# Per-subject projection with residual: loads and stores in one queue in a fixed order

## The reference

```python
def _L0_cond_ref(x, subjects, weights):
    B, C, D, T, N_SUBJECTS = (128, 128, 128, 1024, 8)
    w = weights[subjects]
    out = jnp.einsum('bct,bcd->bdt', x, w)
    return out
x = x + _L0_cond_ref(x, itok_B_0_7, L0_cond_weights)
```

## Time and profile before

| | us |
|---|---|
| median of 3 runs | 324.39 (323.96 to 324.61) |
| the profiled execution | 325.0 |
| its span | 323.2 |
| PE busy | 244.7 (76%) |
| DVE busy | 196.1 (61%) |
| ACT busy | 132.3 (41%) |

### The profile page before, as it was taken

One profiled execution on the slowest core, in us unless ns is written; L12 is line 12 of the kernel. 1 busy time (PEld: TensorE's weight loads), 2 busy tenths in 40 slices (PEclk: granted clock), 3 DMA queues, 4 the chain that ended last, 5 costly groups with the idle time before them and its releaser, 6 DMA issues.

```text
span 323.2 us, 3584 instructions
## 1 busy us (share of the span) xinstructions
PE 244.7 (76%) x1024; PEld 113.0 (35%) x1024; DVE 196.1 (61%) x261; ACT 132.3 (41%) x131; POOL 0.8 (0%) x7
## 2 busy tenths in 40 slices
PE   0599999788868787666996869868668768698640
PEld 0244444343434333333442334434324323344320
DVE  3278888863766755577184773737765547736360
ACT  4045646632434434244152442424443424424240
POOL 1000000000000000000000000000000000000000
PEclk9999999997989999999697998979999979989785
DMA  8999999999999999999999999999999999999994
GB/s 285 422 420 396 431 424 427 428 424 431 426 428 431 423 431 427 425 431 425 431 429 424 431 426 427 432 423 431 427 425 431 425 430 429 424 431 424 428 430 196
DMA packets 17975, 134.80 MB, mean 417 GB/s; under 512 B 1073, under 2 KB 1586, under 8 KB 1586
## 3 DMA queue, kind: packets, MB, share of 16 engines
q1 hardware_dynamic: 9232, 67.64, 50.0%
q10 hardware_dynamic: 8738, 67.11, 49.1%
HBM read 67.63 MB, written 67.11 MB: 417 GB/s over the span
## 4 chain that ended last, share of the span: by engine, by line
DMA 62%; PE 27%; DVEq 2%; DVE 2%; issue 2%; ACT 1%; ACTq 0%; SPq 0%
DMA out<-x_ring 40%; PE product L211 27%; DMA x_ring<-x 21%; DVEq L123 2%; DMA weight_halves<-weights 1%; DVE x_ring L132 1%; DVE x_ring L131 0%; DVEq L44 0%; ACT weight_bank L160 0%; DVE weight_ring L124 0%; ACT x_ring L169 0%; DVE weight_bank L117 0%; DVEq L124 0%; ACTq L187 0%; SPq L81 0%
## 5 line engine op out<-in xcount | busy, mean ns | idle before, releaser
L211 PE MATMUL product<-x_ring,weight_ring 64*128 64x512 f32 x1024 | 244.7, 632 | 66.3 <-DMA x_ring<-x 49.5
L211 PEld LDWEIGHTS product<-x_ring,weight_ring 64*128 64x128 f32 x1024 | 113.0, 200 | 197.2 <-issue 140.1
L131 DVE TENSOR_TENSOR x_ring<-product,x_ring 64x1024 f32<-64x1024 f32 x64 | 77.9, 1217 | 104.3 <-PE product L211 104.3
L168 ACT COPY x_ring<-product 64x1024 f32<-64x1024 f32 x64 | 64.5, 1008 | 176.3 <-PE product L211 176.3
L132 DVE TENSOR_TENSOR x_ring<-product,x_ring 64x1024 f32<-64x1024 f32 x64 | 78.6, 1228 | 0.8
L169 ACT COPY x_ring<-product 64x1024 f32<-64x1024 f32 x64 | 64.2, 1003 | 0.8
L124 DVE COPY weight_ring<-weight_bank 64x256 f32 x128 | 36.9, 288 | 7.1 <-issue 4.3
L111 DVE COPY weight_bank<-weight_halves 64x1024 f32<-64x1024 f32 x2 | 1.4, 688 | 4.8 <-DMA weight_halves<-weights 4.8
L160 ACT COPY weight_bank<-weight_halves 64x1024 f32<-64x1024 f32 x2 | 2.2, 1123 | 2.3 <-DMA weight_halves<-weights 2.3
L160 ACT ACT_TABLE_LOAD x1 | 1.3, 1283 | 1.4 <-PEq L229 1.4
L117 DVE TENSOR_TENSOR weight_bank<-weight_bank,eye 64x512 f32<-64x512 f32 x2 | 1.4, 687 | 0.3 <-ACT weight_bank L160 0.2
## 6 DMA issues: line engine op xcount, KB each, us to landing
x_ring<-x SPq DMA_DIRECT2D x32, 2048.0 KB, 17.2
out<-x_ring ACTq DMA_DIRECT2D x30, 2048.0 KB, 31.2
out<-x_ring ACTq DMA_DIRECT2D x4, 1024.0 KB, 12.2
weight_halves<-weights SPq DMA_DIRECT2D x1, 512.0 KB, 4.2
subject_row<-subjects ACTq DMA_DIRECT2D x1, 0.5 KB
```

What stands on the lines that cost most here:

```text
L131: dve.tensor_tensor(x_ring[LOW, slot, 0, :], low[LOW, :], x_ring[LOW, slot, 0, :], add)
L168: act.copy(x_ring[LOW, slot, 1, :], low[HIGH, :])
L211: last = pe.matmul(product[slot % PRODUCTS][a][:, cols], weight_ring[half, slot, r, :], x_ring[half, slot, r, cols], start=r == 0, stop=r ...
```

## The change

All transfers but the one of the subject numbers are issued by SP, in one queue, in an order that is written out: six loads at once, then for every pair its store, and behind it the load of the pair three further on (`LEAD = 3`, six tiles), as long as there is one to load and it is not among the first six. Before a store SP waits for the pair to be summed and copied; before a load for the store that frees its place. Pair 0 and the last two pairs are stored tile by tile. ACT issues no stores any more. SP, ACT and DVE have no loops; PE keeps its own. DVE reads eight subject numbers (four tiles) into registers with one load, every fourth tile, and has clamped them to 0 to 7 once at the start.

The first piece is SP's instructions before, from the start through the loop to its end. In brackets is what an instruction waits for; `x_out0` is the semaphore of place 0, and 128x2x2048 a pair.

The diff, cut to its core:

```diff
-LOADS_AHEAD = 4
+LEAD = 3
...
+    SINGLE = (*range(PAIR), *range(TILES - REST, TILES))
+
+    def stores(pairs, place):
+
+        return sum(PAIR if (pair * PAIR_SLOTS + place) * PAIR in SINGLE else 1 for pair in range(pairs))
...
         @block.sync
         def _(sp):
-            def load(pair, place):
-                sp.dma_start(x_ring[:, place * PAIR:(place + 1) * PAIR, :, :],
-                             x_of_pair[bass.ds(pair, 1)]).then_inc(x_in[place], DMA_INC)
-
...
-            for place in range(PAIR_SLOTS):
-                if place >= LOADS_AHEAD:
-                    sp.wait_ge(x_in[place - LOADS_AHEAD], DMA_INC)
-                load(place, place)
-            with sp.Fori(1, LAPS) as lap:
-                for place in range(PAIR_SLOTS):
-                    sp.wait_ge(x_out[place], lap * DMA_INC)
-                    load(lap * PAIR_SLOTS + place, place)
-            for place in range(REST // PAIR):
-                sp.wait_ge(x_out[place], LAPS * DMA_INC)
-                load(LAPS * PAIR_SLOTS + place, place)
+            def load(pair):
+                lap, place = divmod(pair, PAIR_SLOTS)
+                if lap:
+                    sp.wait_ge(x_out[place], stores(lap, place) * DMA_INC)
+                sp.dma_start(x_ring[:, place * PAIR:(place + 1) * PAIR, :, :], x_of_pair[pair]).then_inc(x_in[place], DMA_INC)
+
+            def whole(tile):
+
+                sp.wait_ge(copied, tile + (PRODUCTS + 1))
+                sp.wait_ge(summed, tile + (PRODUCTS + 1))
+
+            for pair in range(PAIR_SLOTS):
+                load(pair)
+            for pair in range(PAIRS):
+                place = pair % PAIR_SLOTS
+                if pair * PAIR in SINGLE:
+                    for j in range(PAIR):
+                        whole(pair * PAIR + j)
+                        sp.dma_start(out_of_pair[pair, :, j, :], x_ring[:, place * PAIR + j, :, :]).then_inc(
+                            x_out[place], DMA_INC)
+                else:
+                    whole(pair * PAIR + PAIR - 1)
+                    sp.dma_start(out_of_pair[pair], x_ring[:, place * PAIR:(place + 1) * PAIR, :, :]).then_inc(
+                        x_out[place], DMA_INC)
+                if PAIR_SLOTS <= pair + LEAD < PAIRS:
+                    load(pair + LEAD)
...
-                    subject = dve.value_load(subject_row[0:1, bass.ds(tile * 2 + a, 1)], min_val=0, max_val=S - 1)
...
+                _, numbers = nc.values_load_multi_w_load_instructions(
+                    subject_row[0:1, tile * 2:(tile + PICK_AHEAD) * 2], engines=(mybir.EngineType.DVE,), min_val=0,
+                    max_val=S - 1, skip_runtime_bounds_check_because="DVE has clamped subject_row to 0 .. S - 1")
...
+            dve.wait_ge(subjects_in, DMA_INC)
+            dve.tensor_scalar(subject_row[0:1, :], subject_row[0:1, :], 0, S - 1, mybir.AluOpType.max,
+                              mybir.AluOpType.min).then_inc(clamped, 1)
             dve.wait_ge(weights_in, DMA_INC)
...
-            with dve.Fori(0, LAPS) as lap:
-                for slot in range(SLOTS):
-                    sums(lap * SLOTS + slot, slot)
-                    pick(lap * SLOTS + (slot + PICK_AHEAD), (slot + PICK_AHEAD) % SLOTS)
-            for slot in range(REST):
-                sums(LAPS * SLOTS + slot, slot)
+            for tile in range(TILES):
+                sums(tile, tile % SLOTS)
+                ahead = tile + PICK_AHEAD
+                if ahead < TILES:
+                    if ahead % PICK_AHEAD == 0:
+                        numbers = subjects_of(ahead)
+                    own = ahead % PICK_AHEAD * 2
+                    pick(ahead % SLOTS, numbers[own:own + 2])
...
-                        act.dma_start(out_of_pair[bass.ds(lap * PAIR_SLOTS + place, 1)],
-                                      x_ring[:, place * PAIR:(place + 1) * PAIR, :, :]).then_inc(x_out[place], DMA_INC)
...
+            for tile in range(TILES):
+                cross(tile, tile % SLOTS)
```

More of the change, by code:

```diff
@@ L33, in subject_residual_kernel @@
     PAIRS, PAIR_SLOTS = TILES // PAIR, SLOTS // PAIR
-    assert SLOTS % PAIR == 0 and REST % PAIR == 0 and LOADS_AHEAD < PAIR_SLOTS
+    assert SLOTS % PAIR == 0 and REST % PAIR == 0 and 2 * LEAD <= PAIR_SLOTS
     BANKS = T // PSUM_BANK_COLS
+    SINGLE = (*range(PAIR), *range(TILES - REST, TILES))
+    def stores(pairs, place):
+        return sum(PAIR if (pair * PAIR_SLOTS + place) * PAIR in SINGLE else 1 for pair in range(pairs))
     LOW, HIGH = slice(0, H), slice(H, C)
@@ L57, in subject_residual_kernel @@
         subjects_in = ctx.enter_context(nc.semaphore("subjects_in"))
+        clamped = ctx.enter_context(nc.semaphore("clamped"))
         weights_in = ctx.enter_context(nc.semaphore("weights_in"))
@@ L79, in _ @@
         def _(sp):
-            def load(pair, place):
-                sp.dma_start(x_ring[:, place * PAIR:(place + 1) * PAIR, :, :],
-                             x_of_pair[bass.ds(pair, 1)]).then_inc(x_in[place], DMA_INC)
             sp.dma_start(weight_halves[:, :, :, :],
                          weights.rearrange("(i a) (h r) d -> (a h) i (r d)", a=2, r=R)).then_inc(weights_in, DMA_INC)
-            for place in range(PAIR_SLOTS):
-                if place >= LOADS_AHEAD:
-                    sp.wait_ge(x_in[place - LOADS_AHEAD], DMA_INC)
-                load(place, place)
-            with sp.Fori(1, LAPS) as lap:
-                for place in range(PAIR_SLOTS):
-                    sp.wait_ge(x_out[place], lap * DMA_INC)
-                    load(lap * PAIR_SLOTS + place, place)
-            for place in range(REST // PAIR):
-                sp.wait_ge(x_out[place], LAPS * DMA_INC)
-                load(LAPS * PAIR_SLOTS + place, place)
+            def load(pair):
[21 more added lines that the diff above has]
+                    load(pair + LEAD)
+            for place in reversed(range(PAIR_SLOTS)):
+                sp.wait_ge(x_out[place], DMA_INC * stores(LAPS + (place < REST // PAIR), place))
         @block.gpsimd
@@ L118, in add_eye, with subjects_of, pick @@
                     (H, S, H)), add)
-            def pick(tile, slot):
-                for a, half in enumerate((LOW, HIGH)):
-                    subject = dve.value_load(subject_row[0:1, bass.ds(tile * 2 + a, 1)], min_val=0, max_val=S - 1)
+            def subjects_of(tile):
+                _, numbers = nc.values_load_multi_w_load_instructions(
+                    subject_row[0:1, tile * 2:(tile + PICK_AHEAD) * 2], engines=(mybir.EngineType.DVE,), min_val=0,
+                    max_val=S - 1, skip_runtime_bounds_check_because="DVE has clamped subject_row to 0 .. S - 1")
+                return numbers
+            def pick(slot, numbers):
+                for subject, half in zip(numbers, (LOW, HIGH)):
                     done = dve.tensor_copy(weight_ring[half, slot, :, :], weight_bank[half, bass.ds(subject, 1), :, :])
@@ L144, in _ @@
             dve.wait_ge(eyes_added, 1)
-            dve.wait_ge(subjects_in, DMA_INC)
+            dve.wait_ge(clamped, 1)
+            numbers = subjects_of(0)
             for tile in range(PICK_AHEAD):
-                pick(tile, tile).then_inc(picked, 1)
-            with dve.Fori(0, LAPS) as lap:
-                for slot in range(SLOTS):
-                    sums(lap * SLOTS + slot, slot)
-                    pick(lap * SLOTS + (slot + PICK_AHEAD), (slot + PICK_AHEAD) % SLOTS)
-            for slot in range(REST):
-                sums(LAPS * SLOTS + slot, slot)
+                pick(tile, numbers[tile * 2:tile * 2 + 2]).then_inc(picked, 1)
+            for tile in range(TILES):
[6 more added lines that the diff above has]
+                    pick(ahead % SLOTS, numbers[own:own + 2])
         @block.scalar
@@ L169, in cross @@
                 act.copy(x_ring[HIGH, slot, 0, :], high[LOW, :]).then_inc(copied, 1)
-            def whole(tile):
-                act.wait_ge(copied, tile + (PRODUCTS + 1))
-                act.wait_ge(summed, tile + (PRODUCTS + 1))
             act.dma_start(subject_row[0:1, :], subjects.rearrange("(one b) -> one b", one=1)).then_inc(subjects_in, DMA_INC)
```

## The result

The changed kernel takes 325.12 us (324.56 to 325.91), the kernel before in the same measurement 324.63 us (323.90 to 325.06). The ratio is 1.0020, with a 95% interval of 1.0014 to 1.0026: slower by 0.5 us, where 1.3 us of gain had been forecast. The profiled execution took 325.6 us, its span is 323.8.

The account below looks back on a forecast made before the run. Transfers were taken to bound the kernel: bytes ending at 319.7 us + 0.2 + 0.4 + 0.4 + 1.2 = 321.9 us of span, then + 1.8 - 0.6 = 323.1 us. The range was 321.0 to 327.0, the forecast's own 322.4 to 324.1.

Parts of the forecast that it names:

- The trailing engine: End of the transfers: the 3 us lag belongs to serving two queues, and is valued at 0.2 us in one.
- Rival C: End of the transfers: the trailing engine stays behind, 324.1 to 326.6 us, likeliest 325.6; chance 0.20.
- The rate of one queue: Whole transfer stream: loads at 421 GB/s and stores at 429, together 314.7 us, so bytes end at 319.7 us.
- rival B: Whole transfer stream: engines drift apart, some load while others store, 428 GB/s holds, 320.9 us; chance 0.12.
- The start: First loads and stores: six loads at once worth 0, no dip at 25 to 28 us, queue never dry.
- The steady part: Middle: SP's wait for a summed pair holds back the load behind it, but 8 us of cover makes it cost 0.
- The tail: Last stores behind the last load: a gap before the last half store, 0.4 us, 3.6 at worst.
- Eight subjects to a load: DVE's subject loads, 128 become 16: PE starts 2 to 3 us sooner, but no byte moves earlier; worth 0.
- No loops: DVE's longer program: more of it is fetched by the same DMA engines, between nothing and 1.9 us, taken as 0.4.
- rival D: Queue's 53 turns between store and load: each leaves a gap; at 0.1 us a turn 328.4 us; chance 0.18.

Follow-up runs that it names:

- e7: Kernel before with all computation left out, loads on SP's queue and stores on ACT's: 320.17 us, ratio 0.9868 to before.
- e6: Changed kernel's one queue and order of turns with all computation left out, all transfers of 2 MB: 323.47 us, ratio 0.9968 to before.
- e13: e7 plus PE running its loop of matmuls on a constant array, waiting for no transfer: 321.74 us, ratio 0.9920 to before.
- e4: Changed kernel with PE's loop written out as well, six more program fetches of 16 KB: 324.78 us, ratio 1.0015 to before.
- e14: e7 plus DVE's 120 single loads of a subject number with their copies: 320.71 us, ratio 0.9880 to before.
- e11: Kernel before, two queues, with the loads of subject numbers left out: 323.88 us, ratio 0.9977 to before.
- e5: All computation left out, one queue on SP, all 32 loads and then all 32 stores: 322.63 us, ratio 0.9946 to before.
- e10: e8 with the loads of subject numbers left out, one queue: 325.23 us, ratio 1.0017 to before.
- e3: Changed kernel with LEAD = 4 in place of 3, each load one store further forward: 325.02 us, ratio 1.0019 to before.
- e2: Kernel before with DVE's part of the change alone (no loop, eight subjects to a load, clamp): 324.07 us, ratio 0.9984 to before.
- e16: Repeat of e2, the kernel before with DVE's part of the change alone: 324.05 us, ratio 0.9984 to before.
- e8: Changed kernel with DVE's and ACT's loops and single subject loads of before, so only the queue and order changed: 326.37 us, ratio 1.0050 to before.
- e9: Changed kernel itself, repeated on one chip with e8: 325.26 us, ratio 1.0024 to before.
- e15: e5 with even pairs on SP's queue and odd ones on ACT's, all loads and then all stores: 326.11 us, ratio 1.0048 to before.

## Why the prediction was wrong, by its steps

**The trailing engine is the step that failed.** The prediction read a lag of 3 us at the end of a mixed stretch and no lag in a stretch of loads alone, and took it "that it belongs to serving two queues", 0.2 us in one. e7 has two queues and ends with a lag of 0.2 us, e6 one queue and ends with 2.8. In the changed kernel the lag did not go: it is 4.4 us at 309 us, where the kernel before ends with 3.8. Three sources are seen. Program fetches set single engines back (e13, e4, e14). Turns in one queue let engines drift (e6), so the change itself brought a source. And one engine of the kernel before falls behind evenly while it computes, from 1.1 us at 112 us to 3.4 at 289; what does that is open. e13's 1.6 us are the price of PE and its program; single register loads are worth 0.8 us in the full kernel (e11).

The inference went from one place where several things differed: the number of queues, loads without stores, and almost no program fetches. The first one in the kernel before comes at 22.7 us, near the end of the stretch of loads alone, and the lag goes from 0.5 to 1.1 us there, in one queue. The wrong difference was picked. Rival C said the lag stays; its range (324.1 to 326.6) holds the 325.12 measured.

**The rate of one queue.** The pure rates were right as rates: 422 for loads over 90 us, 428 for stores at first (e5). e5, made of them and without the weights, took 322.6 us. The changed kernel did not run at them but at 427 in the middle. From its 126.69 MB at 300 us, the remaining 8.1 MB at 427 GB/s would end at 318.9 us, so the forecast's 319.7 was 0.8 too long. What was overlooked is the comparison: two queues, undisturbed, stand at 320.2. So the queue's own price is positive, +3.3 us without compute and 1.4 us in the full kernel (e10 less e11). That e6 gets to 428 while its engines drift apart (60 to 166 us) fits rival B's mechanism, engines out of phase so that some load while others store. Then one queue pays either in rate or in lag. The drift is measured; that it is what lifts the rate is argued from the two coming together.

**The start.** Right. The dip went (426 against 352), the queue never ran dry behind the six loads, and none of it moved the end.

**The steady part.** Right: SP's wait for a pair costs nothing, the DMA share is 1.01, the last loads land 9.9 us apart as forecast, and PE waits for loads (56.1 us against the 49.5 of the earlier trace rows):

```profile
PE product L226 <- DMA x_ring<-x: 56.1, 23, 7.8
DVE x_ring L160 <- PE product L226: 112.3, 64, 10.4
```

**The tail.** Mis-sized: 0.4 forecast, 2.2 us of holes found. The latency was right (issued 318.2, bytes from 319, landed 5.1 us after issue), and so was the way from landing to issue (9.9 us, the forecast's value for the fast clock). The cover was not, as a landing is that of the slowest engine, while the others are further on in the queue: 4.3 us at the load of pair 31. The forecast had subtracted no lag from it. So lag and tail are one error: by the rate the bytes would have ended at 318.9 us, and they ended after 322, over 3 us later, where the forecast had 0.2 + 0.4. By e3 the holes are worth nothing alone.

**Eight subjects to a load.** Valued at 0 because DVE had cover. It gained 0.5 us (e2, e16) and 1.1 in one queue (e8 less e9, which differ in ACT's loop too). DVE's cover says nothing about that. It does not come from fewer fetches, for e2 fetches four pieces of 8 KB and the kernel before three; how the loads reach the transfers is open, since e14 does not show it. PE started 1.6 us sooner, not 2 to 3. The 16 loads themselves are longer (median 1345 ns; duration as in the earlier trace rows):

```profile
L145 DVEq TENSOR_LOAD <-subject_row x16: 598/1345/2039, 7.8 to 282.6; - x16
```

**No loops.** 0.4 forecast; e4 with six more fetches shows none that can be measured. The thought behind it, all of a fetch on one engine, was right: 16 KB put an engine back by 0.9 to 1.4 us, but it counts only on the engine that is last.

The sum, by differences of runs on one chip: the queue alone +1.7 us (e8 less before), the new subject loads and ACT without a loop -1.1 (e9 less e8). That leaves +0.6, against the 0.5 measured.

On the number of queues the Trainium skill ("DMA: Bandwidth & Descriptors", rules for kernel authors) holds that issuing from several engines brings no bandwidth. Here it is nearly so: 320.2 against 322.6 and 323.5 us, about 1%, with loads in one queue and stores in the other. With both kinds on both queues there is nothing to gain (e15). The measurements decide.

The Trainium skill's anatomy of one DMA (same page), which the prediction cites in its rival D, is written for transfers that GpSimd (POOL) issues. Here SP and ACT issue them. No run here times what it states; 422 GB/s over 90 us of queued loads (e5) show no standstill between transfers.

## What to carry to other kernels

Where transfers bound a kernel and their queues are full, loads beside stores moved 428 GB/s, loads alone 422 and stores alone 418 to 428; a single queue that takes turns gave up 1% against two. A ragged end (the rate falling to a sixteenth) says that one DMA engine is late. Ask when it fell behind: the increments of each landing tell a step (a program fetch) from a drift. Measure the transfers alone before giving the lag a cause. A landing is that of the last engine, so cover counted from landings is too long by the lag. And when a piece of work is added to a kernel of transfers, look what its program fetches before the work itself is blamed, as with e14.

## What the runs showed of the hardware that was not expected

A program fetch of 16 KB was followed by one DMA engine being 0.9 to 1.4 us further behind (e13, e4, the changed kernel at 35.8 us), one of 8 KB by about 0.6 us (the kernel before at 22.7 us); what is lost so is not made up while the queues are full. Turns between loads and stores in one queue let engines drift apart by 2.8 us (e6) with nothing else running. Leaving out 128 register loads of DVE gained 0.8 us in a kernel bound by transfers (e11). Stores alone went at 428 GB/s for the first 60 us or more in one queue, later at 420, and in two queues at 418 (e5, e15); the reason is open.
